# A two-layer graph transformer on one core: layer 0 sorts ten blocks of targets in place of eight

## The chip, the cores and the metric

The kernel runs on one core of one Trainium2 chip. The metric is the device time of the program in microseconds. The engines are TensorE (PE, with its weight loads as PEld), VectorE (DVE), ScalarE (ACT), GpSimd (POOL) and SyncE (SP, which issues transfers).

## The reference

A graph has 6250 nodes with 128 features and 200000 edges, sorted by target `dst`. Two layers of graph attention (8 heads) follow each other, with one self-loop added for each node. Cut to what matters, a layer is:

```
xn = layernorm(x); xp = xn + xn @ Wpos + bpos + deg * Wdeg + bdeg
q, k, v = xp @ Wq + bq, xp @ Wk + bk, xp @ Wv + bv
att = sum_d(q[dst] * k[src]) / scale, clipped to +-50     # per edge and head
alpha = softmax of att over the edges of one target
x = x + segment_sum(v[src] * alpha, dst) @ Wo + bo
x = x + gelu(layernorm(x) @ W1 + b1) @ W2 + b2
```

The result is `layernorm(x_in + x)`.

## The kernel before

**Two ways to treat edges.** Nodes lie in 49 tiles of 128. Edges, sorted by target, are handled by either of two units. A *chunk* is 1024 edges (8 tiles of 128). Its rows of keys and values are gathered from the table in memory by eight indirect DMAs that GpSimd issues (L1971), into a ring of four buffers; a gather waits until the messages of the chunk four before it are made. 128 nodes need about four chunks. A *block* handles edges without gathers: 7 source tiles times one target tile. All source rows of the 7 tiles are loaded with one plain DMA (L729), and TensorE picks each edge's row with one-hot matmuls (L940 makes the source positions, L952 the rows), which ScalarE copies out of PSUM (L1227, L1238). Seven blocks make one target tile. Before that, the edges of a target tile must be sorted by their source tile; this is a *sort*.

**How much goes which way.** `NBS = 8, 10` gives the number of target tiles (the last of the 49) that layer 0 and layer 1 treat by blocks. `Layer.__init__` works out `jb = NT - nb` tiles by chunks, `ca = 4 * jb + 1` chunks and `ub = 7 * nb` blocks: 165 chunks and 56 blocks in layer 0, 157 chunks and 70 blocks in layer 1. `unit_order` spreads the blocks evenly between chunks, from chunk 17 in layer 0 and chunk 4 in layer 1 (`FIRST_B`).

**What a unit costs each engine.** TensorE makes one-hots of places (L962, L970), spreads the target's queries to the edges (L993 for a chunk, L1026 for a block) and sums the messages by target (L1009, L1042). ScalarE turns the PSUM banks into one-hots (L1227) and takes exponentials (L1260, L1263). VectorE multiplies queries by keys (L1676), reduces to scores (L1685), clips (L1688, L1691), makes messages (L1700) and adds the sums: twice for a chunk (L1726), once for a block (L1731, L1737).

**The order.** No scheduler is at work. Each unit has two slots, and each engine's program walks through the slots in one order: the work of units u+1, u and u-1, then steps of finished nodes (out projection, feed-forward, next layer's q, k, v), then steps of a sort. An engine works strictly in this order, and semaphores join the engines. `sort_steps` puts the steps in slots:

```
for s in range(NBS[0]) if l == 0 else range(NBS[0], NBS[1]):
    if l == 0:
        u = max(u, 2 * at[(s - 1) * OB] - 8 if s else 0)
    else:
        u = max(u, 2 * at[(s - NBS[0]) * 3 * OB])
```

So eight sorts are in layer 0, each ahead of its tile's blocks, and sorts 8 and 9, which only layer 1 uses, are made early in layer 1. A sort's work on VectorE is L1745 to L1823, on TensorE L1057 to L1071. Both layers use the same sorted lists.

Of the kernel before, what the change touches and what calls it, by code (L numbers as in the profile page):

```python
# [72 lines left out]
GELU_TABLES = "gelu_and_others"  # L73


NBS = 8, 10
NB = max(NBS)
JB = NT - NB

SORTED = [*range(NT - NBS[0], NT), *range(NT - NBS[0] - 1, JB - 1, -1)]  # L80

CA = CPT * (NT - min(NBS)) + LAG

# [23 lines left out]
class Layer:  # L107


    def __init__(self, l, before):  # L110
        self.nb, self.first_b = NBS[l], FIRST_B[l]
        self.jb = NT - self.nb
        self.ca, self.ub = CPT * self.jb + LAG, self.nb * OB
        self.units = self.unit_order()
        self.nu = len(self.units)

        self.unit0, self.chunk0, self.part0 = (
            (before.unit0 + before.nu, before.chunk0 + before.ca, before.part0 + before.ub) if before else (0, 0, 0))
        self.chunk_at = [u for u, (what, _) in enumerate(self.units) if what == "chunk"]
        self.block_at = [u for u, (what, _) in enumerate(self.units) if what == "block"]  # L120
        assert all(b - a > 2 for a, b in zip(self.block_at, self.block_at[1:]))

        self.tiles = sorted(range(NT), key=lambda j: (self.last_unit(j), j))
        self.pos = [self.tiles.index(j) for j in range(NT)]
# [117 lines left out]
def sort_steps(l):  # L242
# [3 lines left out]
    slots, u, at = {}, 0, LAYERS[l].block_at  # L246
# [5 lines that stand above are left out]
        for k in range(SORT_STEPS):  # L252
# [1934 lines left out]
```

## Time and profile before

| | |
|---|---|
| time, median of 3 runs | 3657.33 us (3653.97 to 3659.31) |
| span of the profiled execution | 5559.9 us |
| time of the profiled execution beside its span | none is given |
| mean granted clock of TensorE | 0.744 |
| busy: PE, PEld | 3461.6 us, 2666.6 us |
| busy: DVE, ACT, POOL | 2916.7 us, 1771.1 us, 2472.4 us |
| chain that ended last | PE 32%; another core or an unknown queue 30%; DVE 14%; issue 12%; ACT 10% |

The profiled execution took much longer than the timed ones, so shares of its span are to be read with care: durations of single instructions and waits are of use, sums of idle time less so. "issue" is time in which an engine waited for nothing that the profile shows, and "remote" or "another core or an unknown queue" a wait whose releaser isn't seen.

### The profile page before, as it was taken

To read this page: it belongs to the slowest core of one execution; us is meant where nothing else is said; L and a number is where in the kernel's file an instruction comes from. 1 tells how busy PE (TensorE), PEld (TensorE's weight loads), DVE (VectorE), ACT (ScalarE), POOL (GpSimd) and SP (SyncE) were. 2 spreads that over 40 slices of the span, in tenths; PEclk is the share of its full clock that TensorE was granted. 3 is DMA by queue.
4 is the path that set the end of the run, shared out by engine and by line. 5 is a ranking of instruction groups with operands and counts; after the bars stand their busy time and mean duration, and the time that the engine had idled before them with its cause. 6 is when DMAs were issued, how large, how long until landed. Compare 5 with 4: busy or idle time off the path is not lost.

```text
span 5559.9 us, 72300 instructions
## 1 busy us (share of the span) xinstructions
PE 3461.6 (62%) x24196; PEld 2666.6 (48%) x24475; DVE 2916.7 (52%) x6780; ACT 1771.1 (32%) x4391; POOL 2472.4 (44%) x2597
## 2 busy tenths in 40 slices
PE   5834656655665656666566376666666566666666
PEld 4623445444454445444444254455555455545545
DVE  9944545554454545555455354554554454545455
ACT  2301232323333332323234133333333333333334
POOL 1065444444444444444542544445444454444443
PEclk7756777777777777777777677777777777777777
DMA  2133333333333333333332333333333333333332
GB/s 73 49 111 87 88 106 93 102 88 95 102 94 99 94 102 89 104 95 96 107 105 65 106 103 109 108 107 113 96 108 106 108 110 113 111 102 115 109 104 73
DMA packets 404556, 548.28 MB, mean 99 GB/s; under 512 B 78348, under 2 KB 318656, under 8 KB 403988
## 3 DMA queue, kind: packets, MB, share of 16 engines
q0 software_dynamic: 123648, 337.81, 20.9%
q1 hardware_dynamic: 273030, 198.56, 11.9%
q10 hardware_dynamic: 7506, 7.20, 0.4%
q8 instruction: 203, 3.33, 0.2%
q14 instruction: 169, 1.38, 0.1%
HBM read 518.00 MB, written 25.29 MB: 98 GB/s over the span
## 4 chain that ended last, share of the span: by engine, by line
PE 32%; another core or an unknown queue 30%; DVE 14%; issue 12%; ACT 10%; DVEq 0%; SPq 0%; DMA 0%; ACTq 0%
PE psum L952 7%; PE psum L993 4%; PE psum L1009 3%; ACT scratch L1227 3%; PE psum L1042 3%; PE psum L1026 3%; DVE att L1685 2%; PE psum L970 2%; ACT arena L1238 2%; DVE scratch L1676 2%; DVE kv_ring L1394 1%; PE psum L1123 1%; DVE work L1377 1%; DVE scratch L1700 1%
## 5 line engine op out<-in xcount | busy, mean ns | idle before, releaser
L1971 POOL DMA_INDIRECT kv_ring<-kv_table,src_idx x1936 | 1846.4, 954 | 2132.8 <-DVE scratch L1700 1501.1
L1227 ACT ACTIVATE scratch<-psum 128x512 f32<-128x512 f32 x1148 | 649.5, 570 | 2061.3 <-remote 1442.0
L952 PE MATMUL psum<-arena 128*128 128x256 f32 x1764 | 631.5, 486 | 464.2 <-issue 194.2
L1971 POOL DMA_INDIRECT arena<-kv_table,src_idx x640 | 607.8, 950 | 664.6 <-DVE scratch L1700 489.7
L1726 DVE SCALAR_TENSOR_TENSOR arena<-psum,in_block,arena 128x136 f32 x644 | 200.9, 353 | 1286.4 <-remote 1187.3
L993 PE MATMUL psum<-q_win,scratch 64*128 64x128 f32 x5152 | 534.3, 349 | 285.7 <-issue 149.9
L952 PEld LDWEIGHTS psum<-arena 128*128 128x128 f32 x1764 | 372.6, 236 | 621.0 <-issue 319.2
L1009 PE MATMUL psum<-scratch 128*64 128x136 f32 x5152 | 519.1, 330 | 185.4 <-issue 154.2
L993 PEld LDWEIGHTS psum<-q_win,scratch 64*128 64x128 f32 x5152 | 443.2, 243 | 343.1 <-issue 332.5
L1238 ACT COPY arena<-psum 128x512 f32<-128x512 f32 x504 | 265.1, 532 | 986.9 <-remote 524.7
L1685 DVE TENSOR_REDUCE att<-scratch 128x64 f32<-128x1024 f32 (+1 forms) x448 | 525.1, 1172 | 0.1
L1676 DVE TENSOR_TENSOR scratch<-psum,arena 128x512 f32<-128x512 f32 (+1 forms) x412 | 255.4, 646 | 507.4 <-remote 397.5
L1009 PEld LDWEIGHTS psum<-scratch 128*64 128x64 f32 x5152 | 376.8, 161 | 268.6 <-issue 245.6
L1676 DVE TENSOR_TENSOR scratch<-psum,kv_ring 128x512 f32<-128x512 f32 x484 | 313.7, 684 | 264.5 <-remote 182.6
L1026 PE MATMUL psum<-q_win,scratch 128*128 128x128 f32 x1764 | 272.1, 318 | 288.4 <-ACT arena L1238 270.5
L1042 PE MATMUL psum<-scratch 128*128 128x136 f32 x1764 | 309.2, 332 | 3.8 <-ACT work L1326 3.8
L1700 DVE TENSOR_TENSOR scratch<-kv_ring,psum 128x1024 f32<-128x1024 f32 x242 | 292.3, 1208 | 29.4 <-ACT psum L1260 24.2
L1042 PEld LDWEIGHTS psum<-scratch 128*128 128x128 f32 x1764 | 289.6, 238 | 8.6 <-issue 4.5
L1026 PEld LDWEIGHTS psum<-q_win,scratch 128*128 128x128 f32 x1764 | 273.4, 234 | 12.7 <-issue 3.9
L962 PEld LDWEIGHTS psum<-plan_mem,places 128*128 128x128 bf16 x322 | 35.9, 112 | 423.5 <-issue 372.6
L1700 DVE TENSOR_TENSOR scratch<-arena,psum 128x896 f32<-128x896 f32 (+1 forms) x206 | 232.1, 1127 | 9.0 <-ACT psum L1260 7.4
L1731 DVE TENSOR_TENSOR arena<-arena,psum 128x136 f32<-128x136 f32 x108 | 31.9, 295 | 330.6 <-PE psum L1042 200.0
(251 smaller groups left out, 4873.9 us busy)
## 6 DMA issues: line engine op xcount, KB each, us to landing
arena<-kv_table SPq DMA_DIRECT2D x126, 896.0 KB
kv_ring<-kv_table,src_idx POOLq DMA_INDIRECT x1936
q_win<-q_table SPq DMA_DIRECT2D x644, 32.0 KB
work<-kv_table SPq DMA_DIRECT2D x98, 128.0 KB
arena<-kv_table,src_idx POOLq DMA_INDIRECT x640
q_win<-q_table SPq DMA_DIRECT2D x126, 64.0 KB
work<-q_table SPq DMA_DIRECT2D x98, 64.0 KB
kv_table<-work SPq DMA_DIRECT2D x49, 128.0 KB
```

What stands on the lines that cost most here:

```text
L952: mm = e.matmul(to[:, t % 2 * 2 * D:(t % 2 + 1) * 2 * D], hot_source[:, t * P:(t + 1) * P], source_rows[:, t, :], start=True, stop=True)
L993: m = e.matmul(q_edge[h][:, t * P:(t + 1) * P], hotT[n % 2][h * HALF:(h + 1) * HALF, t * P:(t + 1) * P], q_win[h * HALF:(h + 1) * HALF, n ...
L1009: m = e.matmul(to[h * HALF:(h + 1) * HALF], by_edge[:, t * P + h * HALF:t * P + (h + 1) * HALF], msg[n % 2][:, h * T // 2 + t, :], start=t ...
L1026: m = e.matmul(q_edge[f % 2][:, (t - ts[0]) * P:(t - ts[0] + 1) * P], hotT[n % 2][:, t * P:(t + 1) * P], q_win[:, n % 2, :], start=True, s ...
L1042: m = e.matmul(edge_sum(l, u), hot[n % 2][:, t, :], msg[n % 2][:, t, :], start=t == 0, stop=t == last)
L1227: e.activation(to[:, at:at + width], apart[k % 2][:, 0:width], ACT.Relu, bias=1.0, scale=-1.0).then_inc(apart_read, 1)
L1238: e.copy(kv_block[:, ts[0]:ts[-1] + 1, :].rearrange("p t d -> p (t d)"), apart[k % 2][:, 0:len(ts) * 2 * D]).then_inc(apart_read, 1)
L1676: e.tensor_tensor(prod[:, ts[0] * P:(ts[-1] + 1) * P].rearrange("p (t d) -> p t d", d=D), q_edge[f % 2][:, 0:len(ts) * P].rearrange("p (t ...
L1685: e.tensor_reduce(raw_att.rearrange("p t h -> p (t h)"), prod[:, 0:ts * P].rearrange("p (g d) -> p g d", d=HD), AX_X, ALU.add).then_inc(sc ...
L1700: e.tensor_tensor(msg[n % 2][:, 0:ts, 0:D].rearrange("p t (h d) -> p t h d", d=HD), values.rearrange("p t (h d) -> p t h d", d=HD), ex[:, ...
L1726: e.scalar_tensor_tensor(out=row, in0=of_edges, scalar=in_block[:, k, i:i + 1], in1=row, op0=ALU.mult, op1=ALU.add).then_inc(acc_added, 1)
L1971: e.indirect_dma_start(kv[m % RING_KV][:, t, :], None, kv_table[l], bass.IndirectOffsetOnAxis(ap=src_idx[:, c * T + t:c * T + t + 1], axis ...
```

## The change

```diff
-NBS = 8, 10
+NBS = 10, 10
 NB = max(NBS)
 JB = NT - NB
```

Layer 0 now treats 10 target tiles by blocks: it has 157 chunks and 70 blocks, as layer 1 has. All ten sorts are in layer 0. In layer 1 the range of sorts is empty. Everything else follows from the same rules: blocks stand closer together in layer 0, and rows of 165 chunks (`in_block` and others) shrink to 157.

TensorE, layer 0 before, in the early part in which blocks have set in (L993 spreads a chunk's queries, L940 begins a block's source one-hots):

```order
L993 MATMUL psum<-q_win,scratch 128x128 x8
L1109 MATMUL psum<-row_parts,ones_b 128x128
L1110 MATMUL psum<-w_o,work 128x128
L970 MATMUL psum<-places,arena 128x128 x4
L1009 MATMUL psum<-scratch 64x136 x8
L970 MATMUL psum<-places,arena 128x128 x3
L1121 MATMUL psum<-row_parts,ones_b 128x128
L1123 MATMUL psum<-w,work 128x128 x4
L962 MATMUL psum<-plan_mem,places 128x512
L993 MATMUL psum<-q_win,scratch 128x128 x8
L940 MATMUL psum<-arena,places 128x512
L940 MATMUL psum<-arena,places 128x384
```


The same place after the change (L1026 spreads a block's queries):

```order
L1026 MATMUL psum<-q_win,scratch 128x128 x7
L1127 MATMUL psum<-ident,work 128x128
L970 MATMUL psum<-places,plan_mem 128x128 x4
L1009 MATMUL psum<-scratch 64x136 x8
L1106 MATMUL psum<-ident,work 128x128
L962 MATMUL psum<-plan_mem,places 128x512
L993 MATMUL psum<-q_win,scratch 128x128 x8
L940 MATMUL psum<-arena,places 128x512
L940 MATMUL psum<-arena,places 128x384
```


Before, two chunks are spread ahead of the next block's L940; after, one chunk stands between two blocks here.

VectorE, layer 1 before, near its start (L1745 to L1759 are the first steps of sort 8, L1700 makes a chunk's messages):

```order
L1676 TENSOR_TENSOR scratch<-psum,kv_ring 128x512 x2
L1745 TENSOR_SCALAR arena<-arena 128x40
L1746 TENSOR_SCALAR arena<-arena 128x40
L1747 TENSOR_SCALAR arena<-arena 128x40
L1749 TENSOR_SCALAR arena<-arena 128x40
L1750 TENSOR_SCALAR arena<-arena 128x40
L1752 SCALAR_TENSOR_TENSOR arena<-arena 128x40
L1755 SCALAR_TENSOR_TENSOR arena<-arena 128x40
L1700 TENSOR_TENSOR scratch<-kv_ring,psum 128x8x128
L1737 COPY arena<-psum 128x136
L1863 TENSOR_TENSOR work<-work 128x128
L1759 TENSOR_TENSOR arena<-arena,iota_rep 128x1960
```


The same place after:

```order
L1676 TENSOR_TENSOR scratch<-psum,kv_ring 128x512 x2
L1700 TENSOR_TENSOR scratch<-kv_ring,psum 128x8x128
L1737 COPY arena<-psum 128x136
L1863 TENSOR_TENSOR work<-work 128x128
L1685 TENSOR_REDUCE att<-scratch 128x64
```


The eight operations of the sort are gone from this place; they stand in layer 0 now, between the units there.

## Rows read from the trace of the kernel before

**Rows 1.** Busy time of the engines by stretch; columns as in the first line

```profile
core 0: us, PE busy (x) PEld busy (x) DVE busy (x) ACT busy (x) POOL busy (x), PEclk, DMA share, GB/s
0.00:288.20 288.20, 199.68 (x2136) 152.45 (x2136) 264.74 (x478) 76.67 (x161) 27.41 (x23) 0.74 0.23 68
288.20:3053.20 2765.00, 1647.39 (x11152) 1269.27 (x11287) 1394.99 (x3292) 827.08 (x2080) 1255.90 (x1320) 0.73 0.33 95
3053.20:5502.80 2449.60, 1578.78 (x10678) 1216.42 (x10822) 1223.83 (x2902) 839.72 (x2087) 1189.11 (x1256) 0.76 0.36 108
```

**Rows 2.** GpSimd in order of time, four places

```profile
288.18 0.95 POOL L1971 DMA_INDIRECT kv_ring<-kv_table,src_idx  x1 [0.30 <-issue]
289.43 0.95 POOL L1971 DMA_INDIRECT kv_ring<-kv_table,src_idx  x1 [0.30 <-issue]
...
335.09 0.94 POOL L1971 DMA_INDIRECT kv_ring<-kv_table,src_idx  x1 [8.49 <-DVE scratch L1700]
...
3053.18 0.94 POOL L1971 DMA_INDIRECT kv_ring<-kv_table,src_idx  x1 [70.25 <-DMA kv_table<-work]
...
5501.81 0.95 POOL L1971 DMA_INDIRECT kv_ring<-kv_table,src_idx  x1 [0.30 <-issue]
```

**Rows 3.** Waits of GpSimd: us in total, times, longest us

```profile
POOL kv_ring L1971 <- DVE scratch L1700: 1501.1, 198, 17.9
POOL kv_ring L1971 <- issue: 534.0, 1736, 1.2
```

**Rows 4.** TensorE in order of time from 1269.73 us: start, length

```profile
1269.73 1.03 PE L952 MATMUL psum<-arena 128*128 128x256 f32 x4
1270.59 0.86 PE L1042 MATMUL psum<-scratch 128*128 128x136 f32 x6
1271.28 0.59 PE L952 MATMUL psum<-arena 128*128 128x256 f32 x2
...
1271.83 2.52 PE L1063 MATMUL psum<-arena 128*98 128x128 bf16 x10
1274.41 1.72 PE L1026 MATMUL psum<-q_win,scratch 128*128 128x128 f32 x14
1275.97 0.27 PE L1127 MATMUL psum<-ident,work 128*128 128x128 f32 x1
...
1276.65 0.39 PE L970 MATMUL psum<-places,plan_mem 128*128 128x128 bf16 x4
1277.06 1.15 PE L1009 MATMUL psum<-scratch 128*64 128x136 f32 x16
1278.14 0.39 PE L962 MATMUL psum<-plan_mem,places 128*128 128x512 bf16 x1
...
1280.17 0.27 PE L993 MATMUL psum<-q_win,scratch 64*128 64x128 f32 x1 [0.46 <-issue]
```

**Rows 5.** VectorE in layer 0, groups by form: busy us, mean ns, idle before

```profile
L1685 DVE TENSOR_REDUCE att<-scratch 128x64 f32<-128x1024 f32 x165 | 199.5, 1209 | 0.0
L1676 DVE TENSOR_TENSOR scratch<-psum,kv_ring 128x512 f32<-128x512 f32 x248 | 161.5, 684 | 154.7 <-remote 104.8 <-issue 26.0 <-PE psum L993 23.4
L1700 DVE TENSOR_TENSOR scratch<-kv_ring,psum 128x1024 f32<-128x1024 f32 x124 | 150.0, 1210 | 15.5 <-ACT psum L1260 11.4 <-issue 4.0
L1726 DVE SCALAR_TENSOR_TENSOR arena<-psum,in_block,arena 128x136 f32 x330 | 103.0, 353 | 779.6 <-remote 720.0 <-PE psum L1009 50.0 <-issue 9.0
...
L1731 DVE TENSOR_TENSOR arena<-arena,psum 128x136 f32<-128x136 f32 x48 | 14.1, 294 | 114.1 <-PE psum L1042 67.1 <-issue 34.9 <-remote 11.9
```

**Rows 6.** VectorE in layer 0, the costliest groups of the sorts

```profile
L1772 DVE TENSOR_REDUCE arena<-arena 128x10 f32<-128x490 bf16 x32 | 32.8, 1024 | 0.0
L1779 DVE TENSOR_TENSOR arena<-arena,iota_rep 128x1280 bf16<-128x1280 bf16 x32 | 26.2, 819 | 0.0
L1782 DVE TENSOR_TENSOR arena<-arena 128x490 bf16<-128x490 bf16 x64 | 23.4, 406 | 0.0
L1801 DVE TENSOR_TENSOR arena<-earlier,arena 40x490 bf16<-40x490 bf16 x32 | 21.0, 656 | 0.3
L1793 DVE TENSOR_TENSOR arena<-psum,arena 128x490 bf16<-128x490 f32 x32 | 20.9, 654 | 0.0
```

## The prediction

> **What bounds the kernel now.** I read the sums by stage first [rows 1]. The window to 288.2 us is the preparation, the second is layer 0, the third is layer 1 up to its last gather. The span is 5559.9 us, but the timed median is 3657.33 us, so the recording itself costs 1903 us and no engine's share of this span is its share of the real time. The next view to read is therefore TensorE in order of time [rows 4]. Up to 1278 us its groups follow each other without a gap. Then one matmul at a time comes, the one at 1280.17 with 0.46 us of "issue" before it, in the middle of a group that waits for nothing. That is the recording's stall. It hits the engine with most records, and whoever waits for TensorE shows a wait that the timed run need not have.
>
> What the recording leaves alone is GpSimd [rows 2]. One gather starts every 1.25 us (288.18, 289.43): 0.95 us of work and 0.30 us between. The 0.30 us is not a rare case: 534.0 us of such idle time before 1736 gathers is 0.31 us each, the longest 1.2 us [rows 3]. A chunk has eight gathers, so it costs GpSimd 10.0 us. Now the floor that GpSimd sets: preparation 288.2; layer 0 with 165 chunks x 10.0 = 1650; 8.5 us once (ahead of the row at 335.09), while the ring of four is full and no chunk is used yet; 70.3 us between the layers (the row at 3053.18); layer 1 with 157 x 10.0 = 1570; and 5559.9 - 5502.8 = 57.1 us behind the last gather. The sum is 3644 us, 13 us under the median. So I read the timed kernel as paced by the gathers in both layers. The sum is not made against the recorded 5559.9 us: its waits of GpSimd for messages (1501.1 us in one row [rows 3]) are what the recording adds, and I make it against the median, which the floor meets within 0.4%.
>
> VectorE comes next [rows 1]: 1394.99 us busy in layer 0 against 1650 (85%), 1223.83 us in layer 1 against 1570 (78%).
>
> **The change, part by part.** Layer 0 goes from 165 chunks and 56 blocks to 157 and 70, and takes two more sorts. Layer 1 keeps 157 and 70 and loses two sorts.
>
> *GpSimd*: 8 chunks x 8 gathers x 1.25 us = 80 us less. This is the only gain, and it counts if the other engines can follow.
>
> *VectorE, one chunk* [rows 5]: two products 2 x 0.684, reduce 1.209, message 1.210, two additions 2 x 0.353, and two small operations on the scores that I take at 0.4 together (estimate, from the additions, which are larger): 4.9 us. *One block* has seven tiles in place of eight: 7/8 of products, reduce and message (3.79 us), 3.3, one addition 0.294, the small ones 0.4: 4.0 us, and I take 4.1 for their fixed part. *One sort* [rows 6]: its five costliest groups are 32.8 + 26.2 + 23.4 + 21.0 + 20.9 = 124.3 us for eight sorts, 15.5 us each; its smaller steps I take as a third more (estimate): 21 us. Layer 0: -8 x 4.9 + 14 x 4.1 + 2 x 21 = +60 us, so 1395 becomes 1455 us. Layer 1: -42 us.
>
> *TensorE*, by starts, at the granted clock of 2.4 GHz that the fast rows have [rows 4]: a block has 14 records of gathering rows (0.86 us per four, from 1269.73 to 1270.59): 3.0; 14 of spreading queries, 1.56 (1274.41 to 1275.97); 14 of summing, 0.69 per six (1270.59 to 1271.28): 1.6; and three sets of seven one-hots, of 0.41 us per four (1276.65 to 1277.06): 1.9 with some rounding down: 8.1 us. A chunk is 1.08 (1277.06 to 1278.14) for summing, as much for spreading (estimate), and 0.7 of one-hots: 2.9 us. A sort has four groups of ten matmuls that put its values in their slots, at 2.58 us (1271.83 to 1274.41), and I add half as much for its ranks and totals (estimate): 15.5 us. Layer 0: -23 + 113 + 31 = +121 us. Before, TensorE is between 1647 us (as recorded, mean clock 0.73) and 1647 x 0.73 = 1202 us (all of it at full clock). After: 1202 + 121 = 1323 at the low end and 1647 + 121/0.73 = 1813 at the high end. The middle, 1568 us, is just GpSimd's new 1570.
>
> The group at 1269.73 is recorded as 1.03 us long, and the next starts 0.86 us behind it [rows 4], so recorded ends overlap. The Trainium skill says in "Perfetto Trace Analysis", Tensor Engine Instruction, that the recorded end of a matmul is computed from its size, not observed; the rows agree. By recorded lengths the block would be 1.03 x 3.5 + 1.72 + 0.86 x 14/6 + 1.9 = 9.2 us, and TensorE's middle value after the change 15 us higher, over the new 1570; by starts it is 8.1 us and 1568.
>
> *Where the new period ends.* The first block stands behind chunk 17 in both kernels. Ahead of it GpSimd needs 170 us and VectorE only some 130 (17 x 4.9 = 83, one sort 21, and a few nodes, estimate), so that part stays paced by gathers. Behind it, GpSimd needs 1400 us for 140 chunks, where it needed 1480. VectorE is busy there 1455 - 130 = 1325 us, where it was 1265. That is 95% of GpSimd's time, and 100% is not to be had, since each unit passes from TensorE to VectorE and back in both engines' fixed order. The rows price these waits [rows 5]: before a chunk's products and additions VectorE waits for TensorE's L993 and L1009 23.4 + 50.0 = 73.4 us, 0.44 us a chunk. Before a block's addition it waits 67.1 us for L1042 in 48 additions, 1.4 us, or 114.1 / 48 = 2.4 us when all idle time there counts (part of it is the recording's). With 1.4 the blocks' part of the layer is 1325 + 140 x 0.44 + 70 x 1.4 = 1485 us, and layer 0 170 + 1485 = 1655. With 2.4 it is 1555 and 1725. The middle is 1690 against 1650 before: +40 us. The same count for before with 2.4 gives 1265 + 148 x 0.44 + 56 x 2.4 = 1465, under GpSimd's 1480, so it does not contradict a kernel that gathers pace. I take the middle because the idle time named "issue" and "remote" in that row is partly true waiting that the trace couldn't name.
>
> *What is late next*: in layer 0 GpSimd then waits for messages (the ring of four is full), which costs nothing more. The mean share of the DMA engines is 0.33 in layer 0 [rows 1], so the source rows of 14 more blocks find room. No block waits for its sort: by the code's slots the first sort ends 6 units ahead of its first block, the others 13 or more.
>
> *Layer 1*: the two sorts that go lie beside gathers that need 1570 us; VectorE goes from 78% to 75%. If the gathers pace it, nothing comes of it; if not, at most 42 us. I take 10.
>
> Sum: 3657 + 40 - 10 = 3687 us.
>
> **The rivals.**
> *Gathers pace layer 0 still.* For it: VectorE's pure work leaves 5% free, and its waits may be the recording's. Then all 80 us come: 3577 us. Against it: TensorE's middle value also fills the period.
> *The gain is just given back*, 1.4 us a block: 3657 + 5 - 10, 3650 to 3664 us.
> *TensorE is what bounds already, at the recorded prices.* Its busy time in the two layers and the parts around them, 288 + 1647 + 70 + 1579 + 57, is 3641 us, as close to the median as the gathers' floor. A block costs 8.1 / 0.73 = 11.1 us, a chunk 4.0: 14 x 11.1 - 8 x 4.0 = +123; the sorts only move. 3780 us. It decides from the point at which TensorE's mean clock stays near 0.73; against it, the fast rows [rows 4] are shorter than the recorded mean, and a TensorE that is busy all the time has no idle stretch behind which its clock fell.
> *Sorts hold up the gathers.* VectorE's small integer operations and casts, some 12 a sort (by the code), could each keep GpSimd from going on: the longest gap is 1.2 us, 0.9 over the usual, so two sorts more cost at most 2 x 12 x 0.9 = 22 us in layer 0. With gathers pacing, 3577 + 22 = 3599 us. The mean of 0.31 us speaks against it. The Trainium skill's "SBUF — State Buffer", Who interferes with whom, has this as a rule: casts and scalar operations in a two-port mode lock GpSimd out for their whole length. By that rule the gaps during sorts would be longer; the row's mean shows almost nothing of it.
> *Part of both*: the waits shrink to half of 1.4 us a block, so that layer 0 is at 1606 and saves 44, or layer 1 gives its 42: 3600 to 3648 us.
>
> **How the numbers follow.** Forecast 0.46 (its own range 3664 to 3730); gathers pace 0.18; given back 0.12; TensorE bound 0.12; sorts hold up gathers 0.05; part of both 0.07. 0.2% (7 us) is about what the measurement can tell from no change. Faster: 0.18 + 0.05 + 0.07 = 0.30. Same: 0.12. Slower: 0.46 + 0.12 = 0.58. The range reaches down to 3572, so that it holds the gathers' case, and up to 3760, leaving out TensorE's and the upper tail of the forecast, under 2 in 10 together.
>
> **What would show it.** Right: in the profile after, gathers are 64 fewer at the same 1.25 us; VectorE's busy time in layer 0 is near 1455 us; the mean of a block's wait for L1042 is no smaller; the time between the first gather of layer 0 and that of layer 1 does not shrink by 80 us beyond what the recording blurs. Wrong: a time near 3577 means that waits between the two engines vanish when they have no spare time, and my 1.4 to 2.4 us a block were the recording's. A time over 3750 means that TensorE costs what it is recorded at.

## The result, and the profile after

The changed kernel takes 3798.8 us (median of 4 runs, 3794.7 to 3807.09) where the kernel before takes 3657.29 (4 runs, 3653.97 to 3659.31): a ratio of 1.0397, 95% interval 1.0381 to 1.0414, or 141.5 us more. The forecast was 3687, its range ended at 3760, so the sign was right and the size was not. Some executions of a kernel are slowed for their whole length and show a lower granted clock (three of the six of n710 below, 3731 to 3989 us); all times here are of the others.

The kernel before took 3657 us beside the kernel after and 3647 to 3650 us beside the experiments below, so a difference between an experiment's time and 3798.8 can be some 7 us too large. The ratios are each against the kernel before as it ran beside.

This recording did not hold the kernel up: its span is 3792.7 us. The same view as [rows 1], of the changed kernel (preparation, layer 0, layer 1, each cut at a gather):

```profile
0.00:298.10 298.10, 218.22 (x2136) 158.70 (x2136) 265.43 (x478) 75.94 (x161) 22.75 (x22) 0.66 0.21 62
298.10:2174.10 1876.00, 1538.52 (x11905) 1198.10 (x11905) 1432.81 (x3414) 889.47 (x2218) 1210.53 (x1255) 0.88 0.48 144
2174.10:3747.90 1573.80, 1279.14 (x10769) 1003.37 (x10768) 1192.09 (x2843) 842.60 (x2105) 1191.12 (x1256) 0.92 0.56 168
```

A recording of the unchanged kernel taken later (b_again below) was not held up either, with a span of 3645.6 us. It stands in for [rows 1] from here on:

```profile
0.00:288.00 288.00, 205.69 (x2136) 154.69 (x2136) 264.14 (x478) 76.01 (x161) 22.74 (x23) 0.74 0.22 64
288.00:2025.60 1737.60, 1375.00 (x11152) 1085.46 (x11287) 1383.39 (x3292) 823.58 (x2080) 1265.24 (x1319) 0.89 0.51 153
2025.60:3600.10 1574.50, 1277.96 (x10800) 1025.75 (x10944) 1228.04 (x2931) 842.70 (x2109) 1191.51 (x1256) 0.92 0.56 168
```

Layer 1 is the same in both to 1 us, although it lost two sorts and 36 us of VectorE's work (1228 to 1192): its 157 chunks at 10.0 us are 1570 us, so the gathers pace it with or without the two sorts. All of the loss is in layer 0, which grew from 1737.6 to 1876.0 us while its gathers need 80 us less. The rest of the 147 us between the two spans is in the preparation, 10 us. The change does not touch the preparation, and in the recordings of the kernels made from the kernel after it ends at 289 to 300 us, so these 10 us are not put down to the change.

GpSimd's waits in the kernel after, in the form of [rows 3]:

```profile
POOL kv_ring L1971 <- issue: 561.9, 1841, 0.5
...
POOL kv_ring L1971 <- DVE scratch L1700: 161.5, 45, 9.4
POOL arena L1971 <- DVE scratch L1700: 88.0, 14, 11.3
```

The last two rows, 250 us together, are GpSimd waiting until VectorE has made the messages (L1700) of an earlier chunk. Its own 0.3 us between gathers is the same as before. So the gathers no longer pace layer 0; something that ends in VectorE's messages does.

Where in layer 0? Call the stretch from one sort to the next a cycle. The next two rows are one cycle of the kernel after, both cut at messages: the first stretch is 12 units in which a sort's steps stand, the second the 9 units up to the next sort.

```profile
1121.60:1235.10 113.50, 94.51 (x659) 73.34 (x658) 83.47 (x201) 45.24 (x117) 64.39 (x67) 0.82 0.44 129
1235.10:1291.00 55.90, 49.70 (x445) 39.11 (x444) 47.98 (x114) 38.48 (x95) 41.30 (x44) 1.00 0.58 175
```

The same of b_again, 12 units with a sort and the 13 that follow:

```profile
818.20:920.60 102.40, 84.07 (x640) 67.04 (x645) 83.83 (x201) 41.86 (x108) 75.11 (x78) 0.87 0.52 155
920.60:1009.30 88.70, 73.17 (x663) 58.11 (x672) 76.86 (x182) 55.39 (x138) 67.07 (x72) 1.00 0.57 172
```

Read GpSimd's column first. Before, a cycle takes 191.1 us and holds 78 + 72 = 150 records of GpSimd, nearly all gathers, which need 188 us at 1.25. After, it takes 169.4 us and holds 111, which need 139. So a cycle is 30 us over the gathers' pace; nine cycles are 270 us, and layer 0 as a whole is 250 us over it (1824 us from the second to the last gather, for 157 chunks that need 1574). Then read the time of a unit: without a sort 6.2 us, at a clock of 1.00; with one 9.5 us, at 0.82. No engine is at 100% in the slow stretch: PE 83%, DVE 74%. (In b_again a unit without a sort takes 6.8 us, but there the gathers hold it back: 72 records need 90 us.)

TensorE of the kernel after in order of time, in that stretch, in the form of [rows 4]:

```profile
1138.86 3.76 PE L1057 MATMUL psum<-arena,one_tile 128*40 128x49 bf16 x40
1142.55 0.61 PE L970 MATMUL psum<-places,plan_mem 128*128 128x128 bf16 x4
1142.95 2.13 PE L1042 MATMUL psum<-scratch 128*128 128x136 f32 x8
...
1152.56 1.16 PE L993 MATMUL psum<-q_win,scratch 64*128 64x128 f32 x16
...
1158.57 0.28 PE L1113 MATMUL psum<-ident,work 128*128 128x128 f32 x1
1163.13 0.59 PE L1070 MATMUL psum<-arena,before 128*128 128x490 bf16 x1 [4.28 <-DVE work L1871]
...
1164.71 2.08 PE L993 MATMUL psum<-q_win,scratch 64*128 64x128 f32 x16
```

VectorE at the same place:

```profile
1140.15 1.21 DVE L1700 TENSOR_TENSOR scratch<-arena,psum 128x1024 f32<-128x1024 f32 x1
1146.74 0.29 DVE L1731 TENSOR_TENSOR arena<-arena,psum 128x136 f32<-128x136 f32 x1 [5.38 <-PE psum L1042]
...
1159.49 1.01 DVE L1772 TENSOR_REDUCE arena<-arena 128x10 f32<-128x490 bf16 x1
```

The two waits show the same thing from both sides. At 1138.86 TensorE makes the sort's totals, 40 small matmuls, 3.76 us; the block's sums (L1042) stand behind them, and VectorE waits 5.38 us for those. After 1158.57 it is TensorE that has nothing to do: VectorE has a sort's reduction and cast (L1772 and L1774, some 1.2 us), a block's message, a chunk's sums and a node's steps ahead of L1871, and TensorE waits 4.28 us for that. So a sort's step on one engine can stand in the way of the other engine; how much of a sort is paid so is a question for experiments. The granted clock falls too. It is 1.00 up to 1140.6 us, 0.78 from there to 1142.5 and 0.52 to 1145.2, so the 8 records of L1042 take 2.13 us where at 1120.82 they took 1.15. By 1152.56 it is 1.00 again (16 records of L993 in 1.16 us), and behind the second place it is 0.50: the same 16 records take 2.08 us at 1164.71. These are the two levels, 2.4 and 1.2 GHz.

### The profile page after: what moved, and what is told of

The parts are those of the page before. It is cut to its first block, busy times and chain, and to the rows that moved or that the text cites. A ratio compares the mean times of both kernels' runs of the same rounds, so it can differ in the third digit from the quotient of the medians.

```text
span 3792.7 us, 73625 instructions
## 1 busy us (share of the span) xinstructions
PE 3058.1 (81%) x24917; PEld 2377.6 (63%) x24917; DVE 2911.4 (77%) x6814; ACT 1826.7 (48%) x4525; POOL 2425.3 (64%) x2533
## 4 chain that ended last, share of the span: by engine, by line
POOL 34%; PE 25%; DVE 18%; issue 14%; ACT 6%; DMA 2%; DVEq 1%; SPq 0%; POOLq 0%; ACTq 0%
POOL kv_ring L1971 25%; POOL arena L1971 8%; PE psum L952 5%; PE psum L1042 3%; DVE att L1685 3%; PE psum L993 3%; PE psum L1063 2%; PE psum L1009 2%; DVE scratch L1676 2%; DVE work L1377 2%; DVE kv_ring L1394 2%; DVE arena L1726 1%; PE psum L828 1%; ACT arena L1238 1%; PE psum L970 1%
## 5 line engine op out<-in xcount | busy, mean ns | idle before, releaser
L1971 POOL DMA_INDIRECT kv_ring<-kv_table,src_idx x1888 | 1810.7, 959 | 809.6 <-issue 561.9
L1227 ACT ACTIVATE scratch<-psum 128x512 f32<-128x512 f32 (+1 forms) x1188 | 666.1, 568 | 539.8 <-PE psum L962 325.3
L952 PE MATMUL psum<-arena 128*128 128x256 f32 x1960 | 577.5, 415 | 69.6 <-ACT arena L1238 67.0
L1238 ACT COPY arena<-psum 128x512 f32<-128x512 f32 (+1 forms) x560 | 296.7, 532 | 519.7 <-PE psum L952 502.1
L993 PE MATMUL psum<-q_win,scratch 64*128 64x128 f32 x5024 | 414.3, 311 | 117.2 <-DVE scratch L1676 78.8
L993 PEld LDWEIGHTS psum<-q_win,scratch 64*128 64x128 f32 x5024 | 349.8, 211 | 221.7 <-issue 170.3
L1009 PE MATMUL psum<-scratch 128*64 128x136 f32 x5024 | 409.8, 311 | 25.8 <-ACT work L1321 7.3
L1009 PEld LDWEIGHTS psum<-scratch 128*64 128x64 f32 x5024 | 322.0, 151 | 64.7 <-issue 34.4
L1260 ACT ACTIVATE psum<-att 128x64 f32<-128x64 f32 (+1 forms) x454 | 102.7, 226 | 414.4 <-DVE att L1691 407.0
L1042 PE MATMUL psum<-scratch 128*128 128x136 f32 x1960 | 292.6, 293 | 3.3 <-ACT work L1326 3.0
L1700 DVE TENSOR_TENSOR scratch<-kv_ring,psum 128x1024 f32<-128x1024 f32 x236 | 284.8, 1207 | 4.5 <-ACT psum L1260 4.2
L1042 PEld LDWEIGHTS psum<-scratch 128*128 128x128 f32 x1960 | 269.6, 199 | 11.6 <-issue 3.9
L1700 DVE TENSOR_TENSOR scratch<-arena,psum 128x896 f32<-128x896 f32 (+1 forms) x218 | 244.8, 1123 | 18.0 <-ACT psum L1260 18.0
L1026 PEld LDWEIGHTS psum<-q_win,scratch 128*128 128x128 f32 x1960 | 244.9, 195 | 15.5 <-issue 7.6
L1026 PE MATMUL psum<-q_win,scratch 128*128 128x128 f32 x1960 | 246.7, 279 | 2.3 <-DVE scratch L1676 2.3
L1227 ACT ACTIVATE arena<-psum 128x512 f32<-128x512 f32 (+1 forms) x280 | 150.3, 537 | 198.8 <-PE psum L940 190.1
```

Source lines behind the costliest of these rows:

```text
L952: mm = e.matmul(to[:, t % 2 * 2 * D:(t % 2 + 1) * 2 * D], hot_source[:, t * P:(t + 1) * P], source_rows[:, t, :], start=True, stop=True)
L993: m = e.matmul(q_edge[h][:, t * P:(t + 1) * P], hotT[n % 2][h * HALF:(h + 1) * HALF, t * P:(t + 1) * P], q_win[h * HALF:(h + 1) * HALF, n ...
L1009: m = e.matmul(to[h * HALF:(h + 1) * HALF], by_edge[:, t * P + h * HALF:t * P + (h + 1) * HALF], msg[n % 2][:, h * T // 2 + t, :], start=t ...
L1026: m = e.matmul(q_edge[f % 2][:, (t - ts[0]) * P:(t - ts[0] + 1) * P], hotT[n % 2][:, t * P:(t + 1) * P], q_win[:, n % 2, :], start=True, s ...
L1042: m = e.matmul(edge_sum(l, u), hot[n % 2][:, t, :], msg[n % 2][:, t, :], start=t == 0, stop=t == last)
L1227: e.activation(to[:, at:at + width], apart[k % 2][:, 0:width], ACT.Relu, bias=1.0, scale=-1.0).then_inc(apart_read, 1)
```

## The experiments

Theory S, formed from this: the blocks are hidden, and the price is that of a sort, which TensorE and VectorE pay one behind the other. Theory B, from the prediction: each block brings 1.4 to 2.4 us of waits. The layer-0 column at the end of this section is the time from the start of its second gather (the first is recorded as 4.5 to 9.3 us long) to that of its last, in each trace; the gathers' own pace is 10.02 us a chunk, from a_sort1.

**b_again**, the kernel before unchanged.

> The kernel before, unchanged, for a profile in which TensorE is not held up by the recording. Both theories: about 3657 us. Theory S (the sorts are what costs): units within the slots of a sort are well over the rest, near 9 us each against 6.5, and layer 0 from its first to layer 1's first gather is near 1740 us, some 30 us over what the gathers need. Theory B (the blocks are what costs): units within a sort's slots are not over 7.5 us, and the time per unit is even over layer 0.

3647.45 us (one execution). A unit takes 8.5 us in the stretch with a sort and 6.8 us in the other, as theory S has it. Layer 0 takes 1737.6 us up to layer 1's first gather. Its gathers take 1689 us, against 1654 at their pace: before the change layer 0 was already some 35 us over it. The gap between the layers is 48.5 us and the end 45.5, not the 70.3 and 57.1 of the held-up recording.

**a_sort1**, the kernel after with one sort whose lists serve all ten target tiles; **a_sort8** the same with eight.

```diff
-    for s in range(NBS[0]) if l == 0 else range(NBS[0], NBS[1]):
+    for s in range(SORTED_LISTS) if l == 0 else ():
...
+            s = min(s, SORTED_LISTS - 1)
             e.wait_ge(sort_out, 16 * (s + 1))
```

> The changed kernel with 10 blocks of targets in layer 0, but only the first sort is made; all blocks read its list (nine sorts are left out, so the output is not the reference's). Theory S: layer 0 falls back to the gathers' pace, 1570 us for its 157 chunks, and the time to 3550 to 3590 us. Theory B: nine sorts are worth only what VectorE has to do for them beside TensorE's blocks, some 5 us each, and the time stays over 3730 us.

3525.39 us, ratio 0.9661 (0.9639 to 0.9683). With 70 blocks and one sort, layer 0 is at the gathers' pace:

```profile
292.10:1910.90 1618.80, 1293.20 (x10963) 1027.72 (x11113) 1270.52 (x3018) 879.65 (x2200) 1192.47 (x1256) 0.94 0.55 166
```

GpSimd's waits for messages fall from 250 us to 3.7 in the whole kernel, and the chain that ended last is 64% GpSimd where it is 34% in the kernel after. This refutes theory B: the 14 more blocks cost nothing by themselves. VectorE's additions of L1731 wait 44.3 us for L1042 here, 0.7 us for each of the 60, where they wait 155.2 us in the kernel after with the same 70 blocks.

> The changed kernel with 10 blocks of targets in layer 0 and eight sorts in place of ten; the last two tiles' blocks read the eighth list (two sorts are left out). Theory S: each sort costs about 28 us here, so 3799 - 56 = 3743 us. Theory B: 3785 to 3799 us.

3724.73 us, ratio 1.0214 (1.0189 to 1.0238). Seven sorts more than a_sort1 cost 199 us, 28 each, and the last two up to the kernel after cost 74, 37 each, by the medians. In the traces' layer 0 it is 183 us, 26 each, and 67 us, 33 each; the ratios give 67 for the last two as well. Why the last two cost more than the others stays open.

**b_sorts10**, the kernel before with all ten sorts in layer 0, the last two back to back behind the others (`range(NBS[1]) if l == 0 else ()`).

> The kernel before with its 8 and 10 blocks of targets, but all ten sorts in layer 0 (sorts 8 and 9 follow sort 7 back to back, in units 191 to 213) and none in layer 1. It is the part of the change that moves sorts, alone. Theory S: two sorts in a layer with a little room cost 10 to 28 us each and layer 1 gives nothing back: 3677 to 3713 us. Theory B: 3650 to 3665 us.

3680.62 us, ratio 1.0092 (1.0068 to 1.0116): 31 us for two sorts moved, with no block added. Each costs 15 us here and 33 to 37 there. The other reading of this run matters more. It and the kernel after have ten sorts each in layer 0, and differ by 14 blocks in place of 8 chunks: layer 0 takes 1722 us here and 1824 there. So the blocks that cost nothing beside one sort cost 102 us beside ten. It takes both: with 8 chunks fewer the layer's gathers need 80 us less, and that was time under which sorts were hidden. (The run is no pure split, as its last two sorts follow sort 7 back to back.)

**n9**, nine tiles in layer 0 (`NBS = 9, 10`).

> Nine blocks of targets in layer 0 (161 chunks, 63 blocks, nine sorts), ten in layer 1 (one sort left there). If a sort has a price of its own over the gathers' pace in layer 0 and the blocks are hidden, the time lies half way between before and after: 3700 to 3730 us. If there is a threshold (layer 0 has room for one more), it stays at 3620 to 3660 us.

3681.68 us, ratio 1.0095 (1.0071 to 1.012). That is in neither range: there is no free step, and the time is not half way. By the medians the first tile costs 32 us and the second 117, by the ratios 35 and 110: not two equal steps.

**a_pe_lite** and **a_dve_lite** take away the sort's work on one engine each. Of the first, the core of the edit:

```diff
             if name == "totals":
-                for t in range(ST):
+                for t in (0, ST - 1):
...
-                for t in range(RUNS):
+                for t in (0, RUNS - 1):
```

> The changed kernel, all ten sorts, but a sort's TensorE work is cut: 2 in place of 40 matmuls for the totals and 2 in place of 10 for each of the four groups that fill slots (38 + 32 matmuls of a sort left out, so the lists are wrong); VectorE's steps and all waits stay. Theory C (TensorE's part with the fallen clock behind it is most of a sort's price): some 15 us of small matmuls and 10 to 15 us of half clock go per sort, the time falls by 200 us or more, to under 3600 us, and the mean granted clock in the sorts' stretches rises from 0.82 to over 0.9. Theory W (the price is the chain of waits between the two engines and VectorE's work): only the matmuls' own 15 us go, partly hidden: 3670 to 3750 us.

3697.44 us, ratio 1.0129 (1.0105 to 1.0152), 101 us under the kernel after. TensorE's busy time in L1057 to L1071 falls from 174.0 to 66.7 us. The granted clock of the nine stretches with a sort is 0.85 to 0.90, where theory C wanted it over 0.9 and the time under 3600: theory C is refuted.

> The changed kernel, all ten sorts, but from the second sort on VectorE's large steps are cut to 4 of 49 sources and 8 of 128 slots (the lists are wrong); TensorE's matmuls and all waits stay. It takes some 14 us of VectorE's 21 out of a sort. Theory C: TensorE sets the sorts' stretches, so little is gained: 3740 to 3790 us. Theory W: the two parts add up in series, so 9 x 14 us come in full: 3660 to 3690 us.

3706.22 us, ratio 1.0147 (1.012 to 1.0174), 93 us under it. VectorE's busy time in the sorts falls from 210.6 to 99.9 us, 12.3 for each of the nine cut sorts and not 14. That the time lies between the two ranges is in part this. So 107 us less on TensorE bring 101, and 111 us less on VectorE bring 93: most of either engine's work in a sort is paid, and neither is hidden behind the other's.

**a_both_lite**, both cuts.

> The kernel after with both cuts at once (its first sort is whole): 38 of the 40 matmuls of a rank step and 8 of the 10 matmuls of a slots step are left out, and VectorE's large steps of sorts 1 to 9 work on 4 of 49 tiles, so the lists they make are not used rightly and the output differs. The cuts gave 101 us and 93 us alone, of 3798.8. Theory W (a step of VectorE and the next step of TensorE lie behind each other, so the price of a sort is the sum of both engines' work): the cuts add up, 3798.8 - 194 = 3605, range 3580 to 3640, and a stretch with a sort takes 85 to 93 us where it took 113. Theory M (the longer engine alone sets the pace, and each cut only moved the bound to the other one): together they give clearly more than the sum, under 3570, which is where the gathers' pace stands for both layers. Theory H (what is left in either is the wait of a hand-over between units): together clearly less than the sum, over 3650.

(The 40 matmuls that it speaks of are those of the totals step, L1057.) 3617.15 us, ratio 0.9915 (0.9892 to 0.9937): 182 us under the kernel after, where the two cuts alone sum to 194 (180 and some 170 us in the traces' layer 0). Theory W, as it is put here, is right: the two parts lie in series. The stretch with a sort that answers to 113.7 us in the kernel after:

```profile
1349.00:1439.60 90.60, 73.64 (x573) 55.99 (x580) 71.18 (x201) 44.57 (x114) 62.85 (x67) 0.92 0.53 161
```

90.6 us in place of 113.7. Layer 0 is still 70 us over the gathers' pace, from the parts of a sort that stay.

**b_spread**, one free slot more behind each step of a sort that uses a bank.

```diff
             if k in SORT_BANKED:
                 slots.setdefault(u, []).append((s, -k))
+            if l and k in SORT_BANKED:
+                u += 2
+            elif s and k in SORT_BANKED:
+                u += 1
```

> The kernel before, with one free slot more behind each step of a sort that hands over between TensorE and VectorE (two in layer 1); the work is the same. If the waits of the handing over are what a sort costs (theory W), layer 0 gains 5 to 15 us a sort: 3560 to 3620 us. If the work and the clock are (theory C), nothing changes by more than 10 us, or the low clock lasts over a longer stretch: 3640 to 3690 us.

3643.1 us, ratio 0.9983 (0.997 to 0.9995). Where the steps of a sort stand matters by at most 0.3% in the kernel before; whether it does in the kernel after was not tried. Theory W as it is put for this run, that the waits of the handing over are the price, is not borne out: it is how much work the steps are that counts.

**a_fill**, work for TensorE added ahead of the steps, to see what the clock is worth.

```diff
             bank_free(e, m, True)
+            if name != "totals":
+                for _ in range(8):
+                    e.matmul(ps[:, 0:4 * P], ones_b[:], iota_rep[:].rearrange("p b g -> p (b g)")[:, 0:4 * P], start=True, stop=True)
```

> The kernel after with eight matmuls of 128x512 in bf16 more ahead of each rank step and each slots step of a sort, written to the bank that the step itself fills afterwards, so that nothing computed changes. They are 8 x 0.22 = 1.8 us a step if TensorE runs at 2.4 GHz, 14 us a sort with eight such steps, 125 us for nine sorts. Theory K (the granted clock, 0.82 in a stretch with a sort, is part of the price, and TensorE falls to 1.2 GHz because these steps hold it up with little to do): the clock of the stretches rises towards 1, which takes some 15 us of TensorE's 94.5 us back in each, and the time stays near 3800, range 3760 to 3830. Theory N (the clock does not answer to it, or is not part of the price): the added work is paid in full or at half clock, 3880 to 4000.

3829.47 us, ratio 1.0488 (1.047 to 1.0506). The added group and a stretch with a sort in a_fill:

```profile
L1055 PE MATMUL psum<-iota_rep,ones_b 128*128 128x512 bf16 x609 | 159.0, 407 | 49.1 <-DVE work L1874 23.6 <-DVE arena L1796 9.1 <-ACT work L1324 7.3
```

```profile
1486.20:1603.10 116.90, 98.75 (x713) 73.74 (x722) 83.87 (x200) 45.31 (x115) 63.18 (x66) 0.93 0.42 125
```

TensorE got 159 us of work more and the kernel 31 us longer. The same stretch of the kernel after takes 113.7 us at a clock of 0.83; here it takes 116.9 at 0.93 (over all nine such stretches the clock is 0.82 to 0.91 there and 0.92 to 0.98 here). The clock gave part of the 128 us back: those of TensorE's other groups in layer 0 that have as many records in both traces, 1656 us of busy time in the kernel after, are 70 us shorter here. The rest of the 128 us is taken to have stood in time in which TensorE was idle before. Theory N (3880 to 4000) is refuted, and the run came out at the upper edge of what theory K gave. The clock is part of a sort's price; what the whole time would be at an unbroken 2.4 GHz stays open.

**a_vals** and **b_vals**, after and before with the run as the outermost index of `s_vals`, so that TensorE loads neighbouring elements as weights.

```diff
-        s_vals = part_of(RUNS * NT).bitcast(BF16).rearrange("p (v b g) -> p v b g", v=2, g=RUNS)
+        s_vals = part_of(RUNS * NT).bitcast(BF16).rearrange("p (g v b) -> p g v b", v=2, g=RUNS)
```

> The kernel after with one array of a sort (the values that the slots step loads as weights) laid out with the run as the outermost index, so that each of the ten weight loads of a slots step reads 98 neighbouring elements in place of elements 20 bytes apart. They take 252 ns each now, where other loads of the kernel take 112. 400 loads less 140 ns are 56 us, 5.6 a sort, if they stand on the path of the sort; VectorE's two writes of the array (406 ns each) become strided and may get slower, at most to twice: 64 x 0.4 = 26 us lost. Theory W (work of TensorE and VectorE in a sort lies in series): 3750 to 3785. If the loads are hidden behind the matmuls or the recorded 252 ns is no real length: 3795 to 3825.

> The same layout in the kernel before (eight sorts in layer 0, two in layer 1). There layer 0 is over the pace of the gathers by only about 40 us, so a gain from shorter sorts ends at 3610. Theory W: 45 us less on the path of eight sorts, some 26 us more on VectorE at the worst, in sum 3620 to 3650. If the loads are hidden: 3650 to 3670.

3922.88 us, ratio 1.0743 (1.0724 to 1.0762), and 3779.49 us, ratio 1.0343 (1.0324 to 1.0362). I took VectorE's strided writes at twice their time at most. They are 6.3 times as long (a_vals):

```profile
L1782 DVE TENSOR_TENSOR arena<-arena 128x490 bf16<-128x490 bf16 x80 | 189.6, 2573 | 0.0
...
L1063 PEld LDWEIGHTS psum<-arena 128*98 128x98 bf16 x400 | 63.5, 168 | 195.6 <-issue 85.0 <-DVE arena L1793 45.6 <-DVE work L1901 15.9
```

A failed improvement is a good measurement. In a_vals the eight writes of a sort take 8 x (2.573 - 0.406) = 17.3 us more of VectorE, 156 us for the nine sorts behind the first. The weight loads are 84 ns shorter, 40 in a sort, which gives at most 30 us back. That makes 126 us, and 124 us more are measured (134 in layer 0 of the traces): VectorE's work in a sort is paid nearly in full. In b_vals layer 0 takes 102 us more than in b_again, and layer 1 with its two sorts 34 us more, 1608 against 1574, which is both sorts' 17 us in full. So layer 1's sorts were hidden, but with no room to spare.

**n710** (`NBS = 7, 10`) and **n710_spread** (with the edit of b_spread), to find where the two bounds meet.

> The kernel before with seven tiles by blocks in layer 0 (169 chunks, 49 blocks, seven sorts there and three in layer 1). Theory X (layer 0 is bound by whichever is longer, the gathers at 10.0 us a chunk or the work of TensorE and VectorE with some 36 us a sort and some 6.4 us a unit): the gathers need 1690 in layer 0, the compute falls under that, layer 0 stays at 1690 to 1700 where before it was 1689, layer 1 (1570 at the gathers' pace, with room for a third sort) stays, so the whole is within 10 us of before, 3640 to 3660. Theory Y (each tile by blocks costs or gives the same step whatever the gathers do, +32 us from eight to nine, so -32 from eight to seven): 3615 to 3625. If the third sort doesn't fit in layer 1's room: 3670 to 3690.

> The same with a free slot more behind each step of a sort that uses a PSUM bank, as in b_spread (-0.17 per cent there). Layer 0 is at the gathers' pace by theory X, so shorter hand-overs give nothing: within 6 us of n710. If hand-overs still hold up the gathers there: 8 to 20 us less than n710.

n710: 3672.08 us, ratio 1.0065 (1.0046 to 1.0084). n710_spread: 3673.76 us, ratio 1.0075 (1.0059 to 1.0092). A tile less gives nothing back, against theory Y; it costs some 24 us, which is in the range for a third sort that doesn't fit in layer 1. But layer 1 takes only 7 us more than in b_again. Layer 0's gathers take 1708 us, 19 more than there and 14 over their pace of 1694, and the preparation 7 more, which other recordings vary by too. Spreading the steps changes nothing (0.1%, within the intervals), as expected of a layer near the gathers' pace. Of seven to ten tiles, eight is the fastest.

The main ones in one table, in us (layer 0 from its second to its last gather, then what the gathers' pace makes of it, then the first less the second):

| kernel | chunks, sorts in layer 0 | layer 0 | pace | over |
|---|---|---|---|---|
| n710 | 169, 7 | 1708 | 1694 | 14 |
| b_again | 165, 8 | 1689 | 1654 | 35 |
| b_sorts10 | 165, 10 | 1722 | 1654 | 68 |
| n9 | 161, 9 | 1723 | 1614 | 109 |
| a_sort1 | 157, 1 | 1574 | 1574 | 0 |
| a_both_lite | 157, 10 cut on both | 1644 | 1574 | 70 |
| a_dve_lite | 157, 10 cut on VectorE | 1739 | 1574 | 165 |
| a_pe_lite | 157, 10 cut on TensorE | 1740 | 1574 | 166 |
| a_sort8 | 157, 8 | 1757 | 1574 | 183 |
| after | 157, 10 | 1824 | 1574 | 250 |

The last row can be worked out (an estimate, from the rows above). A cycle of the kernel after has 21 units, 14 of them chunks. Without a sort the units need 21 x 6.2 = 130 us, and their gathers 140, so 10 us are free. A sort is 21.1 us of VectorE and 17.4 of TensorE, 38.5 in series, and so 28 us too long; nine cycles make 256 us, and 250 are measured.

## Why the prediction was partly right

**"Paced by gathers in both layers."** Right for layer 1, and nearly for layer 0. The sum of 3644 us was 33 too high, because 70.3 and 57.1 us were read from a recording that held TensorE up; in the one that was not held up they are 48.5 and 45.5. Against 3611 the median leaves 46 us where 13 seemed to be left, and some 35 of them are what layer 0 takes over the gathers' pace. A reader of the floor alone saw no sign that the layer was at its crossing.

**GpSimd -80 us.** The 64 gathers are gone and the others still start 1.25 us apart. The gain is real: a_sort1 shows it.

**VectorE's and TensorE's work.** VectorE's busy time in layer 0 rose by 49 us (1383 to 1433) where 60 was forecast; TensorE's by 164 where 121 was (part of that is the lower clock, since its records get longer). One term was summed too low: 21 one-hots at 0.41 us per four are 2.2 us a block and not 1.9, 4 us for the 14 blocks. The terms of a sort were good too: the trace after has 210.6 us of VectorE in L1745 to L1823 for ten sorts, 21.1 each (forecast 21), and 174.0 us of TensorE in L1057 to L1071, 17.4 each (forecast 15.5).

**"Where the new period ends" is the step that failed.** It took VectorE's work and added waits for each chunk and each block, 0.44 and 1.4 to 2.4 us, but none for a sort. TensorE's 15.5 us were laid beside VectorE's 21, covered by them. The runs put them behind each other: 21.1 + 17.4 = 38.5 us, and the last two sorts cost 33 to 37 each (a_sort8 to after); the two cuts together give 182 us, the sum of each alone is 194. With 15.5 us for each of the nine sorts behind the first, the forecast's own sum gives 140 us more: layer 0 at 1795 to 1865 us in place of 1655 to 1725, and it took 1824. What the forecast blamed, the blocks, costs nothing alone (a_sort1). Their part is that with 8 chunks fewer they took away the time under which sorts were hidden (b_sorts10 against after).

**The wait named for it was real, with another cause.** VectorE's waits for L1042 grew. These are the rows of layer 0, b_again first, the kernel after second:

```profile
DVE arena L1731 <- PE psum L1042: 49.2, 20, 5.1
```

```profile
DVE arena L1731 <- PE psum L1042: 155.2, 57, 7.3
```

In after, the 60 additions of L1731 wait 2.6 us each on average, above my 2.4; in b_again it is 1.0 for each of 48. But it is no property of the block, since with one sort the same 60 wait 0.7 us each (a_sort1). At 1138.86 us L1042 is late because a sort's matmuls stand ahead of it and the clock has fallen.

**The rivals.** "TensorE is what bounds already, at the recorded prices" gave 3780 and came nearest, for the wrong reason. Its mean clock in layer 0 is 0.88, not 0.73: 0.82 to 0.91 in the nine stretches with a sort, 0.94 to 1.00 between them. My argument that a TensorE without idle stretches keeps its clock does not hold either: it fell in the middle of busy time (1140.6 us). A block does not cost 11.1 us of the time: with one sort in place of ten the same 70 blocks run at the gathers' pace. My sign that "a time over 3750 means that TensorE costs what it is recorded at" was therefore wrong. "Gathers pace layer 0 still" (3577) is what the change would give if sorts were cheap. "Sorts hold up the gathers" is refuted: the longest gap named "issue" is 0.5 us in after as in b_again. The rule cited for it, of the Trainium skill's "SBUF — State Buffer", Who interferes with whom, leaves at most 0.2 us over the usual 0.3 in any gap of these rows.

**Layer 1.** I took a gain of 10 us. It was 1: the gathers pace it, as the forecast's other case had it.

## What to carry to other kernels

When one engine's issue rate paces a kernel, work it out for each cycle of the schedule and not for the layer: a burst of work that comes once per cycle is free only while the cycle has room, and the first step past the crossing looks harmless (some 35 us) while the second is not (some 110). Work that two in-order engines hand back and forth is to be added, not laid side by side, until a run with each engine's part cut shows otherwise. And where a recording is far longer than the timed runs, don't take its gaps as terms of a floor: get a recording that isn't held up first.

## What the runs showed of the hardware

- The same program was recorded once with a span of 5559.9 us and once with 3645.6, while its timed medians are at 3647 to 3657. In the long one the busy time of VectorE (2916.7 and 2896.7 us) and of GpSimd (2472.4 and 2480.4) is nearly the same, and TensorE's is 580 us longer (3461.6 and 2881.9).
- A VectorE product of 128x490 in bf16 took 406 ns writing its elements in order and 2573 ns writing them 196 bytes apart. The Trainium skill's "SBUF — State Buffer", Door 1: The DMA port swizzle, says that accesses which leave a 16-byte line pay a penalty. The rows agree in direction; the factor of 6.3 is theirs.
- A weight load of 128x98 in bf16 took 252 ns with elements 20 bytes apart and 168 ns with neighbouring ones.
- TensorE's granted clock fell during or right behind the 40 matmuls of 128x49 (L1057) in six of the ten sorts of the kernel after, although TensorE was busy without a break from the group's start: in the example above from 1.00 to 0.52. In a_pe_lite, with 2 of the 40, it was 1.00 during and behind them in the nine sorts behind the first. Yet the mean clock of the stretches is 0.85 to 0.90 there against 0.82 to 0.91, since it falls behind waits too (0.50 at 1163 us, behind 4.28 us of waiting). Matmuls of 128x512 put ahead of each step raised the clock of such a stretch from 0.83 to 0.93.
